# Attention and mixture-of-experts layer on one core: low halves of the first keys on VectorE, an earlier query split, output weights in four transfers, and one value block more in rounded passes

## The reference, cut to what matters

```
q = rope(x @ w_aq)  k = rope(x @ w_ak)  v = x @ w_av
s = (q * D**-0.25) @ (k * D**-0.25).T       # causal
o = softmax(s) @ v
x1 = layernorm(x + sum over heads of o @ w_ao)
out = layernorm(x1 + routed experts (6 of 64) + shared expert)
```

## Time and profile before

| | |
|---|---|
| median of 3 runs | 1082.75 us (1078.4 to 1085.45) |
| profiled execution | 1081.16 us |
| its span, first to last instruction | 1079.3 us |
| busy in the span | TensorE 974.5 us, VectorE 645.7, ScalarE 487.7, GpSimd 374.3 |
| mean granted TensorE clock | 0.956 |

### The profile page before, as it was taken

The page is one execution under the profiler, slowest core; times in us unless marked ns, Lnnn a source line. Parts: engine busy times, 40 slices in busy tenths (PEclk is TensorE's granted clock), DMA queues, the critical chain, the costliest instruction groups (busy, mean ns, idle before and its releaser), DMA issues.

```text
span 1079.3 us, 16602 instructions
## 1 busy us (share of the span) xinstructions
PE 974.5 (90%) x5192; PEld 731.0 (68%) x5192; DVE 645.7 (60%) x1650; ACT 487.7 (45%) x1083; POOL 374.3 (35%) x335
## 2 busy tenths in 40 slices
PE   8999977999999999999979999999999998549745
PEld 6888866666687877776767666778777776426411
DVE  5987663665657574747656667475757565414326
ACT  4012115545646464545635546464645544126402
POOL 4878972134332212011154322312031112126721
PEclk9999987999999999999989999999999999769968
DMA  8695666463321211112233325351112213988687
GB/s 249 229 288 201 223 225 179 108 166 103 93 76 51 70 45 46 54 32 60 69 120 101 96 65 131 86 155 46 55 31 69 65 58 90 263 228 191 86 264 297
DMA packets 136598, 136.69 MB, mean 127 GB/s; under 512 B 18002, under 2 KB 108230, under 8 KB 136513
## 3 DMA queue, kind: packets, MB, share of 16 engines
q1 hardware_dynamic: 83408, 97.81, 29.8%
q10 hardware_dynamic: 43872, 29.50, 9.4%
q0 software_dynamic: 9232, 8.34, 4.5%
HBM read 86.18 MB, written 62.78 MB: 138 GB/s over the span
## 4 chain that ended last, share of the span: by engine, by line
PE 60%; DVE 12%; DMA 7%; issue 6%; POOL 6%; SPq 5%; ACT 2%; ACTq 1%; POOLq 0%; DVEq 0%
PE s_ps L1114 15%; PE o_ps L1141 11%; PE ring L1124 10%; PE ring L1153 8%; PE o_ps L1144 6%; POOL prods L814 3%; DVE neg_max L1313 2%; SPq L759 2%; DMA qk_rows<-prods 2%; PE ring L1093 2%; DMA sums<-erow,goal_u 2%; SPq L655 1%; DVE prods L1303 1%; DVE prods L1304 1%; PE s_ps L1093 1%
## 5 line engine op out<-in xcount | busy, mean ns | idle before, releaser
L1313 DVE TENSOR_REDUCE neg_max<-s_ps 128x1 f32<-128x128 f32 (+7 forms) x256 | 191.6, 751 | 160.9 <-PE s_ps L1117 159.7
L1114 PE MATMUL s_ps<-kt,qt_hi 128*128 128x512 f32 (+3 forms) x768 | 243.5, 399 | 9.4 <-POOL qt_lo L824 5.8
L959 ACT ACTIVATE probs<-s_ps,neg_max 128x128 f32<-128x128 f32 (+7 forms) x256 | 189.7, 741 | 134.4 <-DVE neg_max L1313 124.4
L824 POOL TENSOR_TENSOR qt_lo<-q_raw,qt_hi 128x512 fp32r<-128x512 f32 x64 | 81.9, 1281 | 324.7 <-ACT qt_hi L873 324.4
L1124 PE MATMUL ring<-ident,probs 128*128 128x128 f32 x1152 | 178.0, 278 | 9.4 <-DVE pt_lo L1251 4.5
L1114 PEld LDWEIGHTS s_ps<-kt,qt_hi 128*128 128x128 f32 x768 | 140.3, 195 | 66.1 <-issue 43.5
L1141 PE MATMUL o_ps<-pt,v 128*128 128x512 f32 x336 | 176.1, 606 | 1.7 <-DVE ot L1334 1.5
L1124 PEld LDWEIGHTS ring<-ident,probs 128*128 128x128 f32 x1152 | 129.4, 143 | 41.0 <-issue 25.9
L970 ACT ACTIVATE pt<-ring 128x512 f32<-128x512 f32 x168 | 99.7, 595 | 95.8 <-PE ring L1124 92.5
L1114 PE MATMUL s_ps<-kt,qt_lo 128*128 128x512 f32 (+3 forms) x384 | 134.6, 350 | 0.0
L844 POOL DMA_INDIRECT slot_rows<-row,slot_u x96 | 95.2, 991 | 95.6 <-DVE slot_u L1438 73.5
(11 more groups left out here) (200 smaller groups left out, 1370.2 us busy)
## 6 DMA issues: line engine op xcount, KB each, us to landing
qk_rows<-prods SPq DMA_DIRECT2D x80, 256.0 KB, 3.0
q_raw<-qk_rows ACTq DMA_DIRECT2D x128, 128.0 KB, 2.9
inv_row<-inverses SPq DMA_DIRECT2D x64, 256.0 KB, 3.4
fsum<-sums SPq DMA_DIRECT2D x48, 256.0 KB, 8.0
sums<-blank SPq DMA_DIRECT2D x16, 640.0 KB, 5.0
wexp<-in_L_ffn_w_gate_dram SPq DMA_DIRECT2D x32, 192.0 KB, 5.3
wexp<-in_L_ffn_w_up_dram SPq DMA_DIRECT2D x32, 192.0 KB, 5.8
wexp<-in_L_ffn_w_down_dram SPq DMA_DIRECT2D x32, 192.0 KB, 6.5
```

The source lines that it names most:

```text
L824: pool.tensor_tensor(qt_lo[:, u % 2, :], q_raw[:, u % QB, :], qt_hi[:, u % 2, :].bitcast(F32), ALU.subtract).then_inc(q_ready, 1)
L959: act.activation(probs[:, u % 2, h, 0:blocks(u) * P], s_ps[:, n % 2, score_cols(n)], ACT.Exp, bias=neg_max[:, n % 8:n % 8 + 1], accum_out= ...
L1114: pe.matmul(s_ps[:, n % 2, c + a:c + e], q[qp], k[kp][:, a:e], start=(qp == kp == 0), stop=(qp == 1 and not last))
L1313: dve.tensor_reduce(neg_max[:, n % 8:n % 8 + 1], s_ps[:, n % 2, score_cols(n)], AX_X, ALU.max, negate=True).then_inc(max_ready, 1)
```

## The change

There are four edits. (1) The low halves of the four key groups of batch 0 are made by VectorE and not by GpSimd. (2) The first two qsplits stand after the rotation of (3, 1, 1) and not of (3, 2, 1), and the ScalarE step at which the first three loads of queries are issued is ("proj", 3, 1, 0, 0) and not ("proj", 3, 1, 1, 0). (3) The output weights are loaded by GpSimd in four transfers, one for each group, behind exp(1, 1), exp(2, 1), exp(3, 1) and exp(4, 1). (4) VF is 2, so the value block j = 2 is handled in three rounded passes as those behind it.

```
-VF = 3
+VF = 2
...
-                if (c, name, a) == (CHUNKS - 1, 2, 1):
+                if (c, name, a) == (CHUNKS - 1, 1, 1):
                     seq += [("qsplit", 0), ("qsplit", 1)]
...
@@ GpSimd
-                if s[0] == "ksplit":
+                if s[0] == "ksplit" and s[1] == 1:
                     b, g = s[1:]
                     pool.wait_ge(k_hi_ready, G * b + g + 1)
...
-                if s == ("exp", 1, 1):
+                if s[0] == "exp" and 1 <= s[1] <= G and s[2] == 1:
+                    g = s[1] - 1
                     pool.wait_ge(proj_ready, PROJ_ALL)
-                    pool.dma_start(wo[:, :, :], w_ao.rearrange("g h d m -> d (g h) m")).then_inc(wo_loaded, 16)
+                    pool.dma_start(wo[:, g * H:(g + 1) * H, :], w_ao[g].rearrange("h d m -> d h m")
+                                   ).then_inc(wo_loaded, 16)
...
@@ ScalarE
-                if s == ("proj", CHUNKS - 1, 1, 1, 0):
+                if s == ("proj", CHUNKS - 1, 1, 0, 0):
                     act.wait_ge(proj_ready, PROJ_AT[("proj", CHUNKS - 1, 0, 1, 1)] + 1)
                     for u in range(QB):
                         load_q(u)
...
@@ TensorE, step outproj; VectorE, first step yadd
-                    pe.wait_ge(wo_loaded, 16)
+                    pe.wait_ge(wo_loaded, 16 * G)
...
-                        dve.wait_ge(wo_loaded, 16)
+                        dve.wait_ge(wo_loaded, 16 * G)
...
@@ VectorE
+                if kind == "ksplit" and s[1] == 0:
+                    g = s[2]
+                    dve.wait_ge(k_hi_ready, g + 1)
+                    low(kt_lo[0][:, g, :], kt_lo[0][:, g, :].bitcast(F32), kt_hi[0][:, g, :]).then_inc(k_ready, 1)
```

## The result

The changed kernel took 1074.38 us (median of 20 runs, 1069.22 to 1081.78), the kernel before, beside it, 1078.24 us (20 runs, 1076.49 to 1085.45). The ratio is 0.9954, with a 95% interval of 0.9935 to 0.9973: 5.0 us less, between 2.9 and 7.0 (the two medians lie 3.9 us apart, the two means 5.0). The time is inside the range on record, and the gain is under the 1% that I called the bound of a measurement here; it is a gain, and about two fifths of the 13 us that I had forecast. The profiled execution took 1073.27 us. The one of before took 1081.16 us, 3 us above the median of its 20 runs, so the pair of profiles (7.8 us of span) shows more than was gained.

What follows compares the result with a forecast made beforehand. It took TensorE's stream and its breaks to bound the kernel. From 1081.2 us it took 9 (edits 1 to 3) and 4 (edit 4), giving 1068, or 1069 for the median; range 1062 to 1078.

Steps and rivals of the forecast that it cites:

- the last rotation: On GpSimd, end of the projections: ends at about 154.8 us, so the next chain starts 4.7 us earlier.
- (a): Rival, chance 0.22: VectorE takes over GpSimd's queue, bank 0 comes free at 148 as now; 1076 us.
- (b): Rival, chance 0.08: last piece of the output weights is late, holding TensorE at the first output projection; 1072 us.
- (c): Rival, chance 0.08: all covers hold, gains of 6.1 + 6 + 6 us; 1064 us.
- (d): Rival, chance 0.07: VectorE becomes the gate of the attention through 48 added subtractions; slower, 1098 us.
- Edit 1: Key low halves, during projections: 9.2 us on VectorE, GpSimd relieved of 5.7 us; gap before first score 2.4 us.
- Edit 2: Query split before the first score: alone only 1.5 us, since VectorE reads bank 0 until 148.0 us.
- The clock: First score to last rotation: 7.5 us would be 5.2 at full clock; 2 us of the 2.3 counted.
- the second break: TensorE from 162 to 168 us, working 3.65 of 6 us at clock 0.72, before the first output projection.
- Edit 3: Reciprocals' chain before the first output projection: 12.4 us become about 8, 4.4 us gained (bounds 0 and 6).
- Edit 4: Attention's matmul stream: 7.7 us off TensorE, 3.8 us of waits, net about 4 us gained.
- The base: The profiled execution of 1081.2 us, with 1.6 us added for the median of the runs shown.

Runs made afterwards that it cites:

- e1: The kernel before with edit 1 alone, key low halves of batch 0 on VectorE; ratio 0.9994 (0.9972 to 1.0016).
- e12: The kernel before with edits 1 and 2, output weights still in one transfer, VF 3; ratio 0.999 (0.997 to 1.001).
- e7: The kernel before with edits 1 and 2, output weights zero in the first output projection and loaded in one transfer after it; ratio 0.9967 (0.9942 to 0.9991).
- e123: The changed kernel without edit 4 (VF 3); ratio to the kernel before 0.9946 (0.9921 to 0.9971).
- e124: The changed kernel without edit 3, output weights in one transfer; ratio to the kernel before 0.9951 (0.9926 to 0.9976).
- e6: The kernel before with value block 2 in three passes but without VectorE's low-half subtraction for it; ratio 0.9957 (0.9936 to 0.9977).
- e2: The kernel before with edit 2 alone, query splits two pairs earlier; ratio 0.9987 (0.9961 to 1.0012).

## Why the prediction was right, and where it was wrong

**The direction and the place were right.** The gain is ahead of the first output projection and, a little of it, in the matmul stream, the gap ahead of the first score shrank, and the last rotation ended at 152.13 + 2.51 = 154.6 us, where I had put 154.8. None of the rivals came: for (a), bank 0 is free by 145.3; for (b), TensorE doesn't wait for `wo` (a piece took 5.0 us to land); for (c), 18 us were not gained; for (d), VectorE's added work costs 2.8 us in the steady stretches and not 33. But the size was off by more than a factor of two, and that the time is in the range is in part luck, as the last paragraph here works out.

**Edit 1: result right, price wrong.** I had VectorE pay 2.3 us for each subtraction and GpSimd 1. VectorE pays 1.21, GpSimd 0.9 to 1.0. I had taken the price from the one row in which VectorE came second, and here it comes first. So the gap fell to 1.47 us and not to 2.4.

**Edit 2: neither borne out nor refuted.** I had it bring only 1.5 us alone, with the time at which the bank is free held fixed at 148.0. That time moves by itself from one execution to the next (147.0 to 149.8 us), and the 2.7 us of edit 2's own profile are hardly outside that scatter. On top of edit 1 it is worth nothing that shows, so it carried nothing of the sum.

**The clock: 2 us counted, 0.7 seen in this profile, 2.3 in others.** I took a gap half as long to keep TensorE at full clock most of the time. In the profiled execution of the kernel after it fell to the lower level for some 3 us behind a gap of 1.47 us, and from the first score to the last rotation it takes 152.13 - 145.31 = 6.8 us instead of 7.5. In e1, e12 and e7, with the same gap, it did not fall, and the stretch takes the 5.2 us that I had worked out for full clock. So the term was sound as an amount, and a matter of chance in each execution. The clock of the second break I had not priced, and there it falls to the lower level in both profiles (0.72 from 162 to 168 us before, 0.55 after).

**Edit 3: 4.4 us predicted, nothing found in the profiles, and this is the step that failed most.** The part on the first unit was right: I had 3 to 4 us for its store, and it took 3.36. I then summed over one unit's chain only. The output projection waits for the chains of four, which share SyncE's queue one behind the other, and the pieces meet each of them. The row in which I might have seen it is in the rows on record: the second L722 came 7.1 us behind the first, the third 4.1 us behind that the earlier trace rows, so one transfer already cost two units and spared the rest. One pair of totals (e12 and e123) speaks for a gain from it and one (after and e124) against, so what edit 3 is worth in the total stays open.

**Edit 4: both terms too large, and one left out.** The 7.7 us for TensorE (48 times the difference of two durations) measured 5.1, and the 3.8 us of waits measured 2.8; net 2.3 and not 4. Of the 0.16 us a block 0.11 was left: in batch 0 of e6 two of the six steps shorten by 0.65 and 0.68 us, which is four times 0.16, and the other four by 0.33 to 0.37, about half of that. What takes the other half there was not looked for. The start of batch 1 takes some 1.5 us back, and I had no term for it: I had put edit 4's side work there (one value block more to store, load and split) at nothing, as lying beside a full TensorE. That it is this work which costs the 1.5 us is likely and not shown. The waits I had spread as 0.08 for each block, while they stand in one tile whose VectorE work has a date to keep.

**The base, and the luck.** I made the sum against the profiled execution and added 1.6 us for the median of three runs. With 20 runs the median of before is 1078.24, which is 2.9 us below the profiled execution and 4.5 us below the median of three. The gain was put at 13 us, and the medians lie 3.9 apart, so the forecast was 9.1 us too low by its gain and 4.5 too high by its base; with 0.8 us lost in rounding (1081.2 - 13 + 1.6 is 1069.8, not 1069) that makes the 5.4 us between 1069 and 1074.4. The range of 1062 to 1078 would nearly have taken in the unchanged kernel at 1078.2, so that the time lies in it says little for the terms. The narrower range of my forecast, 1064 to 1074, was missed by 0.4 us. Rival (d) too is rounded down: its terms make 1099 and not 1098.

## What to carry to other kernels

When work moves between VectorE and GpSimd, ask in which order the two are issued there: whoever comes second pays, so a price must come from a row with the same order. Splitting a transfer that collides with a chain of small ones is worth something only if a piece stays clear of the chain; count the chain over all units that share its queue, not over the first. And for an effect under 0.5%, read the distance between two milestones in a stage that repeats, with a second profile of the unchanged kernel as the scale, before you trust the difference of two profiled totals. Where a stretch does not repeat, one trace says little: compare groups of traces, and do not leave the stretch out of the sum, since a cost can stand in it beside the scatter.

## What the runs showed of the hardware

The long attention stage repeats within 0.1 us in 322 while the whole executions of one kernel scatter over 1% (1069.22 to 1081.78). The scatter of the profiled executions sits outside it: in the first stage, at the start of batch 1, in the last step of the attention and in the experts.

A VectorE subtraction of 128x1024 with both inputs in SBUF took 1.21 us when it started 0.16 us ahead of GpSimd's rotation, which then took 0.9 to 1.0 us longer; the same shape took 2.31 us when GpSimd was already in its rotations.

One step of SyncE's queue, from the reading back of one unit to that of the next, with a small store between them, takes 3.9 to 4.8 us in the trace without a large transfer beside it, and up to 8.0 us (e2) with one, though the queues are different.

And a gap of 1.47 us on TensorE was followed by the lower clock in three traces and by the full clock in three others: in the kernel after it worked 1.53 of 3 us from 143 to 146 and stood at 0.50 from 148 to 150, in e1 it worked 1.60 of 3 us and stood at 1.00.
